# Cross-attention layers 1 and 3 rebuilt: three-part projections, heads on two row halves of TensorE, head-group stacks

## What is computed

```python
h = jnp.concatenate([x, latents], axis=1)
q = (latents @ q_w + q_b).reshape(b, k_len, NH, DH)
kv = (h @ kv_w + kv_b).reshape(b, p + k_len, NH, DH, 2)
kmat, v = (kv[..., 0], kv[..., 1])
attn = jnp.einsum('bkhd,bnhd->bhkn', q, kmat) / DH
attn = jnp.where(full_mask[:, None, None, :], attn, -jnp.inf)
attn = jax.nn.softmax(attn.astype(jnp.float32), axis=-1).astype(q.dtype)
attn_out = jnp.einsum('bhkn,bnhd->bkhd', attn, v).reshape(b, k_len, H)
attn_out = attn_out @ out_w + out_b + residual
```

## Time and profile before

| | us |
|---|---|
| median of 3 runs | 1440.09 (1436.15 to 1443.22) |
| the profiled execution | 1436.25 |
| its span | 1434.4 |
| layer 1, turn and projections (753.7 to 799.2) | 45.5 |
| layer 1, attention (799.2 to 928.3) | 129.1 |
| layer 3, turn and projections (1183.8 to 1230.2) | 46.4 |
| layer 3, attention (1230.2 to 1360.0) | 129.8 |

### The profile page before, as it was taken

How to read it: one execution, slowest core, us unless ns; L and a number is a source line. 1 busy time by engine, 2 the same in 40 slices (tenths; PEclk the granted TensorE clock), 3 DMA queues, 4 the chain that set the end, 5 groups by cost and what they waited for, 6 DMA issues and landing times. The chain is left out here.

```text
span 1434.4 us, 27763 instructions
## 1 busy us (share of the span) xinstructions
PE 1271.2 (89%) x9018; PEld 1027.9 (72%) x9018; DVE 1031.5 (72%) x2398; ACT 704.2 (49%) x1494; POOL 516.7 (36%) x671
## 2 busy tenths in 40 slices
PE   2799999999699999998699799969599949799969
PEld 2699999999599999997595466558377735456558
DVE  5488788887678888877656688575488866688574
ACT  2366566666356666666522255531266612155541
POOL 2654554444455444442203000030299913000030
PEclk7899999999899999999899799989799989799989
DMA  4111100000211001000205444120750015444110
GB/s 153 30 30 31 31 29 22 29 29 1 93 37 31 24 29 29 29 15 0 92 1 179 83 85 84 29 75 1 209 108 2 3 48 178 84 86 84 30 63 30
DMA packets 73867, 79.87 MB, mean 56 GB/s; under 512 B 7908, under 2 KB 59606, under 8 KB 73258
## 3 DMA queue, kind: packets, MB, share of 16 engines
q1 hardware_dynamic: 72904, 78.55, 20.4%
q10 hardware_dynamic: 866, 0.09, 0.0%
HBM read 60.81 MB, written 17.57 MB: 55 GB/s over the span
## 5 line engine op out<-in xcount | busy, mean ns | idle before, releaser
L1756 DVE TENSOR_REDUCE s_mx<-s_s_ps 128x1 f32<-128x512 f32 x256 | 173.0, 688 | 48.0 <-PE s_s_ps L1827 42.6
L1732 ACT ACTIVATE s_probT<-s_st_ps 128x1024 f32<-128x1024 f32 x128 | 129.1, 1024 | 131.3 <-PE s_st_ps L1848 131.0
L742 ACT ACTIVATE a_prob<-a_s_ps,a_negmax 128x257 f32<-128x257 f32 x256 | 119.0, 476 | 99.3 <-DVE a_negmax L832 99.3
L682 POOL TENSOR_TENSOR x_v_hi<-a_v_sum,x_one 128x512 fp32r<-128x512 f32 x64 | 67.4, 1053 | 262.8 <-DVE a_v_sum L821 262.8
L1827 PE MATMUL s_s_ps<-l_k_st,l_q_st 127*128 127x512 f32 x256 | 127.2, 508 | 16.5 <-PEq L1220 13.0
L1506 POOL TENSOR_SCALAR s_below<-s_masked,s_mx 128x256 f32<-128x256 f32 x256 | 117.8, 480 | 29.4 <-DVE s_mx L1534 28.6
L847 DVE TENSOR_TENSOR a_pT_lo<-a_t_ps,a_pT_hi 128x512 fp32r<-128x512 f32 x128 | 88.2, 689 | 36.8 <-ACT a_pT_hi L755 34.8
L832 DVE TENSOR_REDUCE a_negmax<-a_s_ps 128x2 f32<-128x514 f32 x128 | 86.7, 687 | 32.5 <-PE a_s_ps L894 30.7
L1827 PEld LDWEIGHTS s_s_ps<-l_k_st,l_q_st 127*128 127x128 f32 x256 | 51.9, 204 | 77.6 <-DVE s_mx L1756 40.5
L1712 POOL COPY l_v_st<-l_v_all 128x256 f32<-128x256 f32 (+1 forms) x32 | 12.5, 401 | 257.3 <-PE s_o_ps L1859 197.4
L755 ACT ACTIVATE a_pT_hi<-a_t_ps 128x512 fp32r<-128x512 f32 x128 | 76.6, 598 | 55.8 <-PE a_t_ps L948 52.7
(11 more groups left out here) (230 smaller groups left out, 3968.4 us busy)
## 6 DMA issues: line engine op xcount, KB each, us to landing
l_k_st<-k_stack SPq DMA_DIRECT2D x96, 128.0 KB
l_q_st<-q_stack SPq DMA_DIRECT2D x96, 64.0 KB, 2.2
x_wqk_raw<-L_xattn_wq SPq DMA_DIRECT2D x32, 128.0 KB, 2.2
x_wqk_raw<-L_xattn_wk SPq DMA_DIRECT2D x32, 128.0 KB, 2.2
x_wv_raw<-L_xattn_wv SPq DMA_DIRECT2D x16, 256.0 KB, 3.1
a_wo_raw<-L_xattn_wo SPq DMA_DIRECT2D x16, 256.0 KB, 3.3
k_stack<-p_k_hi SPq DMA_DIRECT2D x4, 1024.0 KB, 4.9
k_stack<-p_k_lo SPq DMA_DIRECT2D x4, 1024.0 KB, 5.8
```

The costliest lines, as they stand in the source:

```text
L742: nc.scalar.activation(prob[:, n % 2, qt, 0:NK], s_ps[:, n % 2, qt, 0:NK], ACT.Exp, bias=negmax[:, n % 2, qt:qt + 1], accum_out=den[:, n % ...
L1732: nc.scalar.activation(probT[:, (s + 2) % U, n], st_ps[:, 2 * (n % 2):2 * (n % 2) + 2].rearrange("p k t -> p (k t)"), ACT.Exp).then_inc(z. ...
L1756: nc.vector.tensor_reduce(mx[:, s, n:n + 1], s_ps[:, n % 2, 0:c.NK], AX.X, ALU.max).then_inc(z.max_done, 1)
```

## The change

- Context and state are kept as hi and lo (`c_hi`, `c_lo`, `x_hi`, `x_lo`), the projection weights too (split by ACT and POOL in the MLP before layer 1 and in `final_norm` before layer 3). Keys, queries and values are products of three fp32r matmuls. The transposes of the state move into the projection stage. ACT reads PSUM and adds the bias, DVE makes the lo part in one instruction.
- The stacks in DRAM are laid out head, channel (hi 16, lo 16), batch, token. Rows 0 to 63 of the first 128 channels (heads 0 to 3, "near") are stored first, then rows 64 to 127 ("far"), then the second 128 channels at once ("whole"). A unit, four heads of two batches, is loaded with 8 DMAs; two units are loaded in the projection stage, which ends when all stores and both units have landed.
- In SBUF two heads sit on rows 0 to 49 and two on rows 64 to 113. A score step is two matmuls, one per row half, into two banks; DVE takes two maxima of 512 in one instruction. Transposed scores go in 8 steps of 512 columns through three banks instead of 4 steps of 1024 through two pairs. Values are written directly in the form that TensorE reads, so POOL does no copies. The maxima go as two small DMAs.

```diff
+    def weight_parts(self):
+
+        kv = self.wkv[:].rearrange("p t (n two) -> p t n two", two=2)
+        yield self.wq[:], self.wq_hi[:], self.wq_lo[:]
+        for n in range(2):
+            yield kv[:, :, :, n], self.wkv_hi[:, n], self.wkv_lo[:, n]
+
+    def split_high(self, act, loaded, sem):
+        act.wait_ge(loaded, 48)
+        for raw, hi, _ in self.weight_parts():
+            self.nc.scalar.activation(hi, raw, ACT.Copy).then_inc(sem, 1)
+
+    def split_low(self, pool, sem):
+        for n, (raw, hi, lo) in enumerate(self.weight_parts()):
+            pool.wait_ge(sem, n + 1)
+            self.nc.gpsimd.tensor_tensor(lo, raw, hi.bitcast(F32), ALU.subtract)
...
+def load_unit(c, sp, q_stack, k_stack, q_st, k_st, v, sem):
...
+    HD, (g, part) = c.HD, divmod(v, 2)
+    bs, slot = slice(2 * part, 2 * part + 2), g % 2
+    for half in range(2):
+        heads, at = slice(4 * g + half, 4 * g + 4, 2), half * c.HALF
+        for rows, src in ((slice(at, at + HD), slice(0, HD)), (slice(at + HD, at + 3 * HD), slice(0, 2 * HD))):
+            sp.dma_start(k_st[rows, slot, :, bs].bitcast(F32).rearrange("r a b n -> r a (b n)"),
+                         k_stack[heads, src, bs].rearrange("a r b n -> r a (b n)")).then_inc(sem, 16)
+        for rows, src in ((slice(at, at + 2 * HD), slice(0, 2 * HD)),
+                          (slice(at + 2 * HD, at + 3 * HD), slice(HD, 2 * HD))):
+            sp.dma_start(q_st[rows, slot, :, bs].bitcast(F32).rearrange("r a b t -> r a (b t)"),
+                         q_stack[heads, src, bs].rearrange("a r b t -> r a (b t)")).then_inc(sem, 16)
+    return 8 * 16
...
+        chunks = [(kt, slice(half * 512, (half + 1) * 512)) for half in range(2) for kt in range(KT)]
+        order = [(True, 0), (True, 1), (False, 0)]
+        groups = [(is_k, m, src, half) for m in range(KT) for is_k, src in order for half in range(2)]
+        first_k, first_q = 4, 6
+        tiles = [(src, b) for src in range(2) for b in range(B)]
...
+        def store(sp, is_k, part, m, rows, sem):
+
+            stack, src = (k_stack, (k_hi, k_lo)[part]) if is_k else (q_stack, (q_hi, q_lo)[part])
+            place = part if is_k else 1 - part
+            heads = slice(8 * m + rows.start // c.HD, 8 * m + rows.stop // c.HD)
+            flat = src[rows, m].rearrange("p b s t -> p (b s t)") if is_k else src[rows, m]
+            sp.dma_start(stack[heads, place * c.HD:(place + 1) * c.HD].rearrange("h d b n -> h d (b n)"),
+                         flat.bitcast(F32)).then_inc(sem, 16)
...
+                near, far, whole = slice(0, P // 2), slice(P // 2, P), slice(0, P)
+                for is_k, count in ((True, first_k), (False, first_q)):
+                    for part in range(2):
+                        sp.wait_ge((z.qk_hi, z.qk_lo)[part], count)
+                        store(sp, is_k, part, 0, near, z.stored_first)
+                for is_k in (True, False):
+                    for part in range(2):
+                        store(sp, is_k, part, 0, far, z.stored)
+                sp.wait_ge(z.stored_first, 4 * 16)
+                loaded = load_unit(c, sp, q_stack, k_stack, q_st, k_st, 0, z.first_in)
+                load_unit(c, sp, q_stack, k_stack, q_st, k_st, 1, z.second_in)
+                for is_k, count in ((True, first_q + first_k), (False, 2 * first_q)):
+                    for part in range(2):
+                        sp.wait_ge((z.qk_hi, z.qk_lo)[part], count)
+                        store(sp, is_k, part, 1, whole, z.stored)
+                sp.wait_ge(z.rows_in, 6 * 16)
+                sp.wait_ge(z.first_in, loaded)
+                sp.wait_ge(z.second_in, loaded)
+                sp.wait_ge(z.stored, 8 * 16)
...
+                def product(out, left, right, start, stop):
+
+                    (a_hi, a_lo), (b_hi, b_lo) = left, right
+                    nc.tensor.matmul(out, a_hi, b_hi, start=start, stop=False)
+                    nc.tensor.matmul(out, a_hi, b_lo, start=False, stop=False)
+                    return nc.tensor.matmul(out, a_lo, b_hi, start=False, stop=stop)
...
+                    wait(pe, z.qk_lo, g - 3)
+                    if src or not is_k:
+                        pe.wait_ge(z.x_lo_done, KT * (half + 1))
+                    parts = (x_hi, x_lo) if src or not is_k else (core.c_hi, core.c_lo)
+                    rows, cols = slice(m * P, (m + 1) * P), slice(half * 512, (half + 1) * 512)
+                        left = ((core.wkv_hi[:, 0, kt, rows], core.wkv_lo[:, 0, kt, rows]) if is_k else
+                                (core.wq_hi[:, kt, rows], core.wq_lo[:, kt, rows]))
+                        mm = product(qk_ps[:, g % 4], left, [x[:, kt, cols] for x in parts], kt == 0, kt == KT - 1)
+                    mm.then_inc(z.qk_done, 1)
+                for n, (src, b) in enumerate(tiles):
+                    wait(pe, z.v_out, n - 3)
+                    parts = ((core.c_hi, core.c_lo), (x_hi, x_lo))[src]
+                    for j in range(QT):
+                        tok = slice((QT * b + j) * P, (QT * b + j + 1) * P)
+                        for kt in range(KT):
+                            mm = product(turned[:, n % 4, j * D:(j + 1) * D], [x[:, kt, tok] for x in parts],
+                                         (core.wkv_hi[:, 1, kt], core.wkv_lo[:, 1, kt]), kt == 0, kt == KT - 1)
+                    mm.then_inc(z.v_done, 1)
...
+                    nc.scalar.activation(places(q_hi, k_hi, g), qk_ps[:, g % 4].rearrange("p (b t) -> p b t", t=S),
+                                         ACT.Identity, bias=bias(g)).then_inc(z.qk_hi, 1)
...
+                    nc.vector.scalar_tensor_tensor(out=places(q_lo, k_lo, g),
+                                                   in0=qk_ps[:, g % 4].rearrange("p (b t) -> p b t", t=S),
+                                                   scalar=bias(g), in1=places(q_hi, k_hi, g).bitcast(F32),
+                                                   op0=ALU.add, op1=ALU.subtract).then_inc(z.qk_lo, 1)
...
+    pe_steps = steps("S0 E0 E1 S1 M0 E2 E3 P0 P1 E4 E5 S2 P2 P3 S3 E6 E7 X0")
+    act_steps = steps("E0 E1 E2 E3 E4 E5 O0 E6 E7")
+    dve_steps = steps("M0 S0 S1 S2 S3 X0")
...
+        for i in range(c.quads + 3):
+            body(quad(i), quad(i - 1), quad(i - 2), quad(i - 3))
...
+                def load(v):
+                    wait(sp, z.st_done, NE * 2 * (v - 3))
+                    load_unit(c, sp, q_stack, k_stack, q_st, k_st, v, unit_in[v % 4])
+
+                def body(first, second, third, fourth):
+                    if first == 0:
+                        load(2)
+                        load(3)
+                    if second is not None:
+                        g, b = batch(second)
+                        sp.wait_ge(z.mx_out, second + 1)
+                        for half in range(2):
+                            m = half * HALF + c.MAX_ROW
+                            sp.dma_start(q_st[m:m + 1, g % 2, :, b].bitcast(F32),
+                                         mxT[2 * half:2 * half + 2, second % 2].bitcast(F32)
+                                         ).then_inc(row_in[second % 2], 16)
+                    if first is not None and first >= 4 and first % 2 == 0 and first // 2 + 2 < units:
+                        load(first // 2 + 2)
...
+                def scores(n, i):
+                    g, b = batch(i)
+                    if n == 0 and b % 2 == 0 and i >= B:
+                        v = i // 2
+                        pe.wait_ge(unit_in[v % 4], per_unit * (v // 4 + (v % 4 > 1)))
+                    wait(pe, z.max_done, NS * i + n - 1)
+                    a, qt = n // QT, n % QT
+                    for half in range(2):
+                        q, k = tiles(half, c.MAX_ROW, i)
+                        mm = nc.tensor.matmul(s_ps[:, n % 2, half], q[:, a, qt * P:(qt + 1) * P], k[:, a],
...
+                        pe.wait_ge(row_in[i % 2], 32 * (i // 2 + 1))
+                    u = NE * i + n
+                    wait(pe, z.exp_done, u - 2)
+                    a, pair, half = n // 4, n // 2 % 2, n % 2
+                    q, k = tiles(half, c.MAX_ROW + 1, i)
+                    for j in range(2):
+                        kt = 2 * pair + j
+                        mm = nc.tensor.matmul(st_ps[:, u % 3, j * S:(j + 1) * S], k[:, a, kt * P:(kt + 1) * P], q[:, a],
...
+                        pe.wait_ge(z.exp_done, NE * (i + 1))
+                        wait(pe, z.x_out, i)
+                        pe.wait_ge(z.mx_out, min(i + 3, c.quads))
...
+                        a, half, at = j // 2, j % 2, kt % 2 * S
+                        mm = nc.tensor.matmul(ox_ps[32 * j:32 * j + 32, 0], v_st[:, b, kt, 4 * g + j],
+                                              probT[:, i % 2, a, kt // 2, half, at:at + S],
+                                              start=(kt == 0), stop=(kt == NKT - 1))
...
+                        elif kind == "M" and second is not None:
```

(15 more changed lines are left out.)

552 lines of the change are left out of this document (178 added, 374 removed).

## The result

The changed kernel takes 1470.68 us (median, 1468.73 to 1473.55) against 1439.62 for the kernel before: ratio 1.0222, 95% interval 1.0199 to 1.0246. It is slower, as forecast, and inside the range, but by 31 us instead of 11 to 15.

What follows compares the result with a forecast made beforehand. TensorE was taken as the bound, in the projections followed by the way through DRAM. From 1436.25, +45.4 for projections, +2 for final_norm, -33.7 for attention and +1 for the first rows gave 1451 us, range 1428 to 1485.

Steps and rivals of the forecast that it cites:

- all engines carry the stores: Rival for the projection stores: every DMA engine takes part, windows become 37 us, time 1388; chance 9%.
- the number of partitions decides: Rival for the projection stores: 64 rows use half the engines, 128 all; windows of 43 us, time 1400; chance 5%.
- 8.4 + 1.3 + 57.7 + 0.8: Projection window: first store ready, time to full share, 1.33 MB per busiest engine at 23 GB/s, landing and next stage.
- the loads at a share of 0.84: Projection stores: loads beginning with 16 channels reach 0.84, so few partitions do not halve the share; outermost count does.
- TensorE's sum of 6.2: Attention round: score steps 1.4, transposed 1.85 or 1.6, values 2.0, X0 0.5, M0 0.3, array changes 0.4; range 5.6 to 6.8.
- the halves run one after the other: Rival for the attention: row halves do not overlap, 1.3 us more a round, 33 for both layers, time 1484; chance 7%.
- DVE's loop: Attention round: maxima, PE's transposes of them and M0 wait on each other in a chain of 6.0 us.
- The first row of maxima is queued behind two units in round 1: Attention start: the row waits behind unit loads, costing +0.5 us for each layer, up to 1.5.
- so nothing more for that: Attention start: TensorE begins at the lower clock level as it does now, so no added time.
- 2 taken out of 0 to 3.9: final_norm: POOL's three weight splits beside DVE's bound chain cost up to 3.9 us if DVE waits for the same memory; 2 taken.
- which delays two small row loads by 1.4, needed 5 us later: nothing: final_norm: SP issues the projection weights first, delaying two row loads by 1.4 us, at no cost.
- Nothing for the MLP and the removed work: Splits in the MLP before layer 1 (up to 1 us) and POOL's removed zeroing and value copies: no change in time.

Runs made afterwards that it cites:

- e1_merged: Changed kernel with hi and lo rows of a channel side by side in the DRAM stacks, so stores begin with 64 or 128 rows: 1424.48 us, ratio 0.9903 to the kernel before.
- f1_wide: e1_merged with the near and far stores of 64 channels put together into whole ones of 128 channels: 1426.16 us (one run).
- g_scores: Changed kernel with both matmuls of each score step reading the first half of the rows, transposed steps unaltered: 1523.06 us (one run).
- f3_act: Changed kernel with the rows of maxima issued by ACT on its own queue, SP loading units 2 and 3 as before: 1496.48 us (one run).

## Why the prediction was right or wrong

**The cause, right.** The slowdown came from the DRAM stores being confined by their outermost count, at the share forecast (0.25, then 0.5), and e1_merged takes it away. The rivals "all engines carry the stores" and "the number of partitions decides" fall for the engines: the share followed the heads in three kernels (4 and 8; and 64 and more, which took all).

**The projection windows, right in mechanism, 1.8 and 2.6 short.** Forecast 68.2 = 8.4 + 1.3 + 57.7 + 0.8, and 69.1 in layer 3. Measured in layer 1: the first store moves at 762.0, 9.2 after the transposes; the DMAs end at 822.0; the next stage begins 0.8 later. The mis-sized term is the 57.7, measured 60.0. It took the busiest engines to finish together, but after 816 the share falls from 0.5 by steps (0.38, 0.34, 0.34, 0.26, 0.11, 0.05 in the last six microseconds); had the eight ended together, that rest would have taken 3 us instead of 6, by an estimate from these shares. Layer 3's window is 1.8 longer than layer 1's, where the forecast said 0.9; 1.5 of it are the transposes at the lower clock (3.43 against 1.94).

**A reading that was wrong and cost nothing here.** I took the loads at a share of 0.84 as proof that few partitions don't slow a DMA. The share says how many engines are occupied, not what they move: the same row has 181 GB/s where the stores had 379. With four or eight engines at 106 to 207 GB/s this second limit was hidden; e1_merged ran into it, and so the windows of 37 us in the rival "all engines" were 10 us too short each. How much of the 10 is the stores' rate and how much the loads' no run separates; f1_wide, with fast stores, won back only 0.7 and 3.7 of it.

**The round, right.** 6.2 forecast, 6.00 measured, 6.06 and 6.12 on the mean over twelve rounds, since a row now and then waits for a unit (a round of 6.77 in layer 1). The terms hold: score steps 0.33 for 0.34, the pair of value steps 1.0, maxima 1.13 to 1.17 from start to start for 1.13 to 1.22. TensorE's sum of 6.2 has the transposed steps at 1.6, with overlap (with 1.85 it would be 6.45), and they took 1.6. The rival "the halves run one after the other" falls by the two matmuls of a score step, which lie on top of each other, and by g_scores; its price of 1.3 a round is 1.2 by its own terms (4 x 0.23 + 0.25). That DVE's loop sets the 6.00 is argued only: the last maximum ends at 885.0, PE's S1 and M0 follow at 885.09 and 885.62, DVE's negation at 886.04, and TensorE itself waits but 0.16.

**The start of the attention, wrong: the step that failed.** "The first row of maxima is queued behind two units in round 1: +0.5 for each layer (up to 1.5)." It cost 5.5 in layer 1 (29.9 against 24.4) and 3.8 in layer 3 (29.5 against 25.6): 8.3 more than forecast, nearly half of the 17.8 us that it missed. I had counted 6.5 us for a unit and set it against a steady round, where it is hidden; at the start there are two at once, 2.36 MB at 155 GB/s, all of TensorE's transposed work stands behind the row, and nothing else is left to do. f3_act shows that the wait is mostly for the engines, not for the place in the queue: 3.57 of the 4.97 stayed on a queue of the row's own. Over layer 1's stage: 29.9 up to round 3's copy (forecast 23.2), 72.8 for twelve rounds (74.4), 16.1 for the rest (15.5). Sum 118.8 against 113.1. In layer 3, 1.0 more comes from its window of before, which I had taken that much too long (to 1360.0, where the next stage began at 1359.04).

**The lower clock at the start, put at nothing.** The forecast had the attention start at the lower clock level "as it does now after its shorter pause", "so nothing more for that". It stayed there for 29.2 us of layer 1's stage, against 16.5 before. What that costs by itself is not shown; it may be what is left of the start, 1.2 and 2.4 us.

**final_norm, wrong in size.** 2 taken out of 0 to 3.9; measured 2.8 for DVE beside POOL. And "which delays two small row loads by 1.4, needed 5 us later: nothing" was wrong: they landed 1.3 too late.

**Nothing for the MLP and the removed work, right**: all else is -1.1.

## What to carry to other kernels

Write the address order of a DRAM store so that its outermost dimension is large: 4 gave a share of 0.25, 8 gave 0.5, 64 and 128 gave 1. Then look at GB/s beside the share, since 64 channels moved 221 GB/s and 128 moved 418 with all engines busy. A small transfer that a whole chain waits for must be issued ahead of the bulk ones; a queue of its own doesn't help while their packets fill the engines. Price such waits in the first round, not in the steady one.
